# Attention of a two-layer transformer: query halves outermost, totals over three, three and two key tiles, two output buffers

## The reference

```python
scores = jnp.einsum('bhqd,bhkd->bhqk', q, k) / np.sqrt(HD)
attn = jax.nn.softmax(scores, axis=-1)
out = jnp.einsum('bhqk,bhkd->bhqd', attn, v)
x = residual + out @ wo + bo
x = x + gelu(norm(x) @ ff_w1 + ff_b1) @ ff_w2 + ff_b2
```

## Time and profile before

| | us |
|---|---|
| median of 3 runs | 4369.27 |
| lowest, highest | 4364.93, 4376.75 |
| the profiled execution, its own time | 4378.7 |
| its span, first to last instruction | 4376.9 |

### The profile page before, as it was taken

The page is one execution under the profiler, slowest core; times in us unless marked ns, Lnnn a source line. Parts: engine busy times, 40 slices in busy tenths (PEclk is TensorE's granted clock), DMA queues, the critical chain, the costliest instruction groups (busy, mean ns, idle before and its releaser), DMA issues.

```text
span 4376.9 us, 53519 instructions
## 1 busy us (share of the span) xinstructions
PE 3913.1 (89%) x20400; PEld 1527.1 (35%) x20400; DVE 2427.8 (55%) x3944; ACT 1618.2 (37%) x2807; POOL 1636.8 (37%) x907
## 2 busy tenths in 40 slices
PE   6978899898998989989899998998899898989999
PEld 4312343233432234322243223432244223432234
DVE  3756635655455644556454666366554665556652
ACT  1456313553125531255411553135521553125521
POOL 2367212573115732156410563026510563115620
PEclk9889999989999999999999999999899999999999
DMA  4232242221422123232122021311122112310112
GB/s 133 59 90 107 69 106 73 68 62 56 102 74 64 54 78 91 76 80 67 67 87 87 15 65 57 105 37 42 37 87 92 28 35 71 100 57 18 62 55 95
DMA packets 140701, 307.44 MB, mean 70 GB/s; under 512 B 20336, under 2 KB 60292, under 8 KB 139552
## 3 DMA queue, kind: packets, MB, share of 16 engines
q10 hardware_dynamic: 50944, 174.62, 12.5%
q1 hardware_dynamic: 89504, 129.40, 11.3%
HBM read 225.56 MB, written 36.72 MB: 60 GB/s over the span
## 4 chain that ended last, share of the span: by engine, by line
PE 67%; DVE 13%; DMA 8%; POOL 5%; issue 4%; ACT 2%; SPq 1%; ACTq 0%; POOLq 0%; DVEq 0%
PE ps L774 11%; PE ps L775 11%; PE ps L776 11%; PE ps L954 8%; PE ps L875 7%; PE ps L937 6%; PE ps L811 6%; DMA dcopy<-inverses 5%; DVE mcol L1434 5%; PE ps L969 3%; POOL sums L691 3%; PE ps L828 2%; DMA inverses<-inverse 2%; ACT probs L1116 1%; DVE turn L1356 1%
## 5 line engine op out<-in xcount | busy, mean ns | idle before, releaser
L691 POOL TENSOR_TENSOR sums<-probs 128x1024 f32<-128x1024 f32 x480 | 1141.9, 2392 | 1513.4 <-ACT probs L1116 998.3
L1434 DVE TENSOR_REDUCE mcol<-ps 128x1 f32<-128x512 f32 x2048 | 1284.8, 684 | 543.1 <-PE ps L875 541.3
L1116 ACT ACTIVATE probs<-ps 128x512 f32<-128x512 f32 x2048 | 1105.0, 604 | 905.2 <-PE ps L937 614.4
L937 PE MATMUL ps<-qs,ks 98*128 98x512 f16 x2048 | 800.1, 402 | 190.0 <-ACT probs L1116 188.0
L875 PE MATMUL ps<-ks,qs 97*128 97x512 f16 x2048 | 809.7, 401 | 104.3 <-DVE mcol L1434 72.2
L954 PE MATMUL ps<-probs,v_sb 128*32 128x512 f32 x4096 | 597.2, 659 | 0.0
L1262 ACT ACTIVATE sums<-ps,cols 128x512 f32<-128x512 f32 x256 | 175.8, 687 | 1127.2 <-PE ps L776 1127.2
L875 PEld LDWEIGHTS ps<-ks,qs 97*128 97x128 f16 x2048 | 205.2, 100 | 723.3 <-DVE mcol L1434 385.9
L1520 DVE CAST probs<-sums 128x512 f16<-128x512 f32 x256 | 123.7, 483 | 501.8 <-ACT sums L1262 501.3
L774 PE MATMUL ps<-aT,ring 128*128 128x512 f16 x1024 | 392.2, 383 | 0.0
L775 PE MATMUL ps<-aT,ring 128*128 128x512 f16 x1024 | 391.2, 382 | 0.0
(11 more groups left out here) (106 smaller groups left out, 3221.9 us busy)
## 6 DMA issues: line engine op xcount, KB each, us to landing
ring<-halves ACTq DMA_DIRECT2D x208, 512.0 KB, 3.4
qs<-hl SPq DMA_DIRECT2D x192, 128.0 KB, 4.0
ring<-halves SPq DMA_DIRECT2D x48, 512.0 KB, 6.1
ring<-in_weights ACTq DMA_DIRECT2D x39, 512.0 KB, 4.4
halves<-ring ACTq DMA_DIRECT2D x37, 512.0 KB, 2.9
dcopy<-inverses SPq DMA_DIRECT2D x64, 256.0 KB
ks<-hl SPq DMA_DIRECT2D x120, 128.0 KB, 4.3
probs<-in_x SPq DMA_DIRECT2D x8, 1024.0 KB, 6.7
```

Source lines behind the costliest of these rows:

```text
L691: pool.tensor_tensor(sums[:, m % SUM_SLOTS, :, :], prob(u - 2), prob(u), ALU.add).then_inc(sum_set[0].sem, 1)
L937: pe.matmul(ps[:, bank, :], ks[0:K_EXP, key_set(i, hh), key_head(i, hh, h), P * kt:P * kt + P], qs[0:K_EXP, qc, h, :], start=True, stop=Tr ...
L1116: act.activation(prob(u)[:, e, :], ps[:, w % SCORE_BANKS, :], ACT.Exp).then_inc(exp_done.sem, 1)
L1434: dve.tensor_reduce(mcol[:, blk % 2, 4 * j + qt, half:half + 1], src, AX.X, ALU.max).then_inc(n_free[0], 1)
```

## The change

- Blocks: the query half is outermost, then the head half, then the group. Output tiles 0 to 3 (queries of the first half) then need blocks 0 to 3 only, and start at step 54 instead of 55. The second head half is needed by block 2 instead of 4, the second query half by block 4: fills, rotations and stacks move accordingly. Set 0 of the keys is used until block 5, so `load_again` moves from unit 68 to 98 and the bias additions behind it.
- Sums: over key tiles 0 to 2, 3 to 5 and 6 to 7. The first addition of a slot adds two tiles, the second adds the third one in place; 10 additions a block, 80 an iteration (75 on POOL, 5 on DVE), 3 groups of totals a block, 24 an iteration.
- `ocopy` has two buffers. `normalise` comes after addition 7 of 10, ACT's `finish` after score 11 and POOL's after addition 1, both of the block after that.
- The last block's sums are inverted by DVE in `dcopy` itself, 128 x 512, with no DMA. Forward steps: output tiles 4 to 7 at 2 and 3, norm of their half at 4, finish of blocks 6 and 7 at 0 and 1.

```diff
-O_AT, D_AT, HI_AT, INVERT_AT = 7, 12, 27, 4
+PROBS, SUM_SLOTS, SUMS, GROUPS = 6, 3, 80, 24
+SUM_KT = (1, 2, 4, 5, 7)
+O_AT, D_AT, HI_AT, INVERT_AT, NORM_AT, LO_AT = 7, 12, 11, 4, 7, 1
-WO_AT = 55
-LN2_AT = 62
-BIAS_AT = (40, 41, 42, 43, 48, 49, 54, 55)
-ROTATE_AT = ((1, 2, 6), (5, 6, 16), (14, 15, 31), (26, 28, 59))
+WO_AT = 54
+LN2_AT = 61
+BIAS_AT = (62, 63, 64, 65, 66, 67, 70, 72)
+TURNS = ((("k", 1, 0), -1, 1, 5), (("k", 1, 1), 3, 4, 11), (("q", 0, 1), 13, 17, 29), (("q", 1, 1), 33, 35, 57))
 def block_of(blk):
-    hh, r = divmod(blk, 4)
-    return hh, r // 2, r % 2
+    qc, r = divmod(blk, 4)
+    return r // 2, qc, r % 2
 def sum_of(u):
-    return 8 * (u // 16) + 2 * (u % 16 // 4) + u % 2
+    return 10 * (u // 16) + 2 * (0, 0, 1, 2, 2, 3, 4, 4)[u % 16 // 2] + u % 2
 def sum_unit(m):
-    return 16 * (m // 8) + 4 * (m % 8 // 2) + 2 + m % 2
+    return 16 * (m // 10) + 2 * SUM_KT[m % 10 // 2] + m % 2
+def sum_opens(m):
+    return m % 10 // 2 != 1 and m % 10 // 2 != 3
+def sum_buffer(m):
+    return 6 * (m // 10) + 2 * (0, 0, 1, 1, 2)[m % 10 // 2] + m % 2
 def fills_of(i):
-        for step, key in ((1, ("k", i, 1, 0, 0)), (2, ("k", i, 1, 0, 1)), (3, ("v", i, 1, 0)), (4, ("v", i, 1, 1)),
-                          (5, ("k", i, 1, 1, 0)), (6, ("k", i, 1, 1, 1)), (8, ("v", i, 1, 2)), (9, ("v", i, 1, 3))):
+        for step, key in ((0, ("k", i, 1, 0, 0)), (1, ("k", i, 1, 0, 1)), (2, ("v", i, 1, 0)), (3, ("k", i, 1, 1, 0)),
+                          (4, ("k", i, 1, 1, 1)), (6, ("v", i, 1, 1)), (7, ("v", i, 1, 2)), (9, ("v", i, 1, 3))):
 def narrow_forward(i, n):
-        if n in (3, 4):
-            keys += [("wo", i, 2 * n - 2), ("wo", i, 2 * n - 1)]
+        if n in (2, 3):
+            keys += [("wo", i, 2 * n), ("wo", i, 2 * n + 1)]
...
-        ocopy = sb("ocopy", [P, D], F32)
+        ocopy = sb("ocopy", [P, 2, D], F32)
             def attention(i):
-                        if s == 9:
+                        if s == 7:
                             put_stack(("k", i, 1, 1, 0))
             def forward(i):
-                totals_out(i, 7)
-                inverse_in(i, 7)
...
             def add_probs(i, m):
-                u = sum_unit(m)
+                u, n = sum_unit(m), sum_buffer(m)
                 pool.wait_ge(exp_done.sem, exp_done.at(i, 2 * u + 2))
+                dst = sums[:, n % SUM_SLOTS, :, :]
+                if sum_opens(m):
+                    if n >= SUM_SLOTS:
+                        pool.wait_ge(d_mul.sem, d_mul.at(i, (n - SUM_SLOTS) // 2 + 1))
...
+                    pool.tensor_tensor(dst, prob(u - 2), prob(u), ALU.add).then_inc(sum_set[0].sem, 1)
+                else:
+                    pool.wait_ge(*sum_done(m - 2, i))
+                    pool.tensor_tensor(dst, dst, prob(u), ALU.add).then_inc(sum_set[0].sem, 1)
             def attention(i):
-                    if m == 56:
+                    if m == 69:
                         deviation("ln2", i, 0)
-                    if m >= 8 and m % 8 == 3:
-                        normalise(i, m // 8 - 1)
-                    if m >= 8 and m % 8 == (4 if m // 8 == 6 else 5):
-                        finish(i, m // 8 - 1)
+                    if m >= 10 and m % 10 == NORM_AT:
+                        normalise(i, m // 10 - 1)
+                    if m >= 20 and m % 10 == LO_AT:
+                        finish(i, m // 10 - 2)
             def out_tile(key):
-                pe.wait_ge(at_lo.sem, at_lo.at(i, 6 if tt < 4 else 8))
+                pe.wait_ge(at_lo.sem, at_lo.at(i, 4 if tt < 4 else 8))
             def o_copy(i, blk):
-                if 8 * i + blk >= 1:
-                    act.wait_ge(at_lo.sem, at_lo.at(i, blk))
+                if 8 * i + blk >= 2:
+                    act.wait_ge(at_lo.sem, at_lo.at(i, blk - 1))
             def attention(i):
-                    if u == 68:
+                    if u == 98:
                         load_again(i)
+            def invert_last(i):
+                dve.wait_ge(d_out.sem, d_out.at(i, 8))
+                dve.reciprocal(dcopy[:, :], dcopy[:, :]).then_inc(inv_last.sem, 1)
```

More of the change, by code:

```diff
@@ L144, in first_fills @@
         at = (10, 11, 13, 14, 16, 17, 19, 20, 12, 15, 18, 21)
-        keys = [(kind, j, 0, th, part) for kind in "kq" for th in range(2) for part in range(2)]
+        keys = [("k", j, 0, th, part) for th in range(2) for part in range(2)]
+        keys += [("q", j, hh, 0, part) for hh in range(2) for part in range(2)]
         keys += [("v", j, 0, e) for e in range(4)]
@@ L149, in first_fills @@
         keys = [("k", j, 0, 0, 0), ("k", j, 0, 1, 0)]
-        keys += [("q", j, 0, th, part) for th in range(2) for part in range(2)]
+        keys += [("q", j, hh, 0, part) for hh in range(2) for part in range(2)]
         keys += [("v", j, 0, e) for e in range(2)]
@@ L950, in values @@
                     pe.wait_ge(o_out.sem, o_out.at(i, u // 16))
-                if u == 64 and layer(i) == 0:
+                if u == 32 and layer(i) == 0:
                     pe.wait_ge(*freed(("v", i, 1, 3)))
@@ L956, in values, with totals @@
                 mm.then_inc(v_mul.sem, 1)
-            def totals(i, m):
+            def totals(i, group):
+                m, first, last = last_of(group), group % 3 == 0, group % 3 == 2
                 for k in range(2):
                     pe.wait_ge(*sum_done(m + k, i))
-                if m == 0:
+                if group == 0:
                     if i >= 1:
@@ L993, in attention @@
                         values(i, u - LAG)
-                    m = sum_of(max(u - LAG_D, 0))
-                    if u >= LAG_D and u - LAG_D == sum_unit(m):
-                        totals(i, m)
+                    for group in range(GROUPS):
+                        if u - LAG_D == sum_unit(last_of(group)):
+                            totals(i, group)
                     some(rows_at(i, s))
@@ L1101, in finish @@
                     act.wait_ge(hi_read.sem, hi_read.at(i, blk + 1))
-                    hi = act.activation(ocopy[:, :], ocopy[:, :], ACT.Identity, bias=bias_)
+                    hi = act.activation(ocopy[:, blk % 2, :], ocopy[:, blk % 2, :], ACT.Identity, bias=bias_)
                 hi.then_inc(at_hi.sem, 1)
@@ L1212, in attention @@
                             d_copy(i, blk - 1)
-                        if w % 32 == HI_AT:
-                            finish(i, blk - 1)
+                    if blk >= 2 and w % 32 == HI_AT:
+                        finish(i, blk - 2)
                     if w % 4 == 2:
@@ L1499, in attention @@
                         output_sum(i - 1, 3 + s)
[L1500 removed]
+                    for m in range(10 * blk, 10 * blk + 10):
                         if by_vector(m) and sum_unit(m) // 2 == s:
```

142 lines of the change are left out of this document (74 added, 68 removed).

## The result

The changed kernel takes 4211.31 us (median of 4 runs, 4204.08 to 4214.03) against 4368.16 us for the kernel before beside it (4364.93 to 4376.75): ratio 0.9635, 95% interval 0.9617 to 0.9654, so 157 us faster. I had forecast 4130, a range of 4015 to 4280, and 240 us of gain. The sign, the range and the main mechanism held; a third of the gain didn't come. The profiled execution took 4214.03 us (span 4212.2) against 4378.7 before, 164.7 less.

What follows compares the result with a forecast made beforehand. It took PE to bound attention steps, except once a block POOL's wait for the DMA chain. Gains of 4 x 24 + 4 x 34 + 8 = 240 us took the profiled 4378.7 to 4138.7; it said 4130, range 4015 to 4280.

Steps and rivals of the forecast that it cites:

- Normalising late: In attention blocks, multiplying four units later removes POOL's wait for the inverse; the long last step falls from 6.77 to 2.84 us.
- Nobody waits for the moved multiplication: With the second ocopy buffer finish runs one block later; the next o_copy needs only the finish of two blocks ago.
- Fewer totals: 56 us, all on PE's path if PE stays the limit: Attention steps: 64 fewer groups of totals at 0.87 us of PE each, 56 us in all.
- the slot wait: At a plain block's second addition POOL idles 2.4 us for a slot, making about 28.8 us a block.
- Layer 1's blocks 0, 6, 7: These layer 1 blocks were put at 27.5, 32.3 and 34 us; the whole layer at 24 us less an iteration.
- Layer 0: Its eight blocks were to sum to 280 us against 314.06, 34 us less an iteration.
- The turn to the forward part: After the last block, DVE inverts in place in 4.2 us; net gain 1 us an iteration.
- DVE beside POOL: In attention, longer POOL work was charged nothing for slowing DVE; the shared-port rule would cost up to 19 us.
- A (PE alone): Rival: PE alone limits and POOL's idle time vanishes in its lag; 392 us gained, 3977 us; chance 0.12.
- B: Rival: a second slot wait and late stacks, bias and inverse in layer 0; 120 us gained, 4250 us; chance 0.13.
- C: Rival: the wait for the inverse was hidden anyway, only PE's totals count; 56 us gained, 4313 us; chance 0.07.
- D: Rival: POOL's three slot openings a block each wait 3.1 us; 92 us slower, 4461 us; chance 0.06.

Runs made afterwards that it cites:

- experiment 1: The changed kernel with POOL's normalising multiplication after addition 4 of a block instead of 7: 4367.67 us, ratio 0.9999 to the kernel before.
- Experiment 2: The kernel before (one ocopy buffer, heads outermost) with only the multiplication moved later, its remainder and output tiles shifted to make room: 4460.19 us, ratio 1.0215.
- pairs: The changed kernel with totals over pairs of key tiles again (64 additions, 32 groups an iteration), everything else kept: 4164.13 us, ratio 0.9540.
- Experiment 5: The changed kernel with DVE's ln2 norm of the first half moved behind its additions, one step later: 4222.95 us, ratio 0.9650.
- experiments 4: The changed kernel with ACT rounding layer 0's last rotated query stack after unit 59 instead of 57: 4200.38 us, ratio 0.9605.
- experiment 6: The changed kernel with layer 0's maxima of block 2 starting at step 9 instead of 8 and run denser after: 4208.98 us, ratio 0.9616.
- 12: Pairs with later rotation, tiles apart and later maxima, plus layer 1's output tiles at steps 51, 52, 53, 55 and POOL's deviation one addition earlier: 4146.73 us, ratio 0.9484.
- experiment 7: The changed kernel with output tiles 0 to 3 in steps 53, 55, 56, 57 instead of 54 to 57: 4188.49 us, ratio 0.9570.
- experiment 8: The changed kernel with DVE's four output sums in layer 1's block 0 at steps 0, 3, 3, 6 instead of 1 to 4: 4212.90 us, ratio 0.9639.

## Why the forecast was right in sign and its gain half too large

**Normalising late: right.** L742 idles 2.5 us for the broadcast (I allowed 80), the 6.77 step is gone, plain blocks took 26.75, 28.18 and 27.88 against 28.8. By experiment 1 it is worth 157 us, the whole difference of the two kernels. What the order of the blocks and the second buffer bring by themselves wasn't tried.

**"Nobody waits for the moved multiplication": right, but my reason was incomplete.** I named the o_copy. Experiment 2 shows that ACT's finish, whose move in the diff I hadn't costed, is the nearer waiter: 303.5 us.

**"Fewer totals: 56 us, all on PE's path if PE stays the limit": wrong, with its sign.** The condition failed. I had computed 26.5 us of work for POOL against 26.1 for PE and added the slot wait, and so charged POOL's period in plain blocks; there it fits. But I kept the 56 us as a gain and read the extra additions only there. With pairs a plain block is 26.8, so the grouping *costs* 1.1 to 1.4 us in blocks 4 and 5, where it was modelled, and gains nothing in block 2. In blocks 0, 6 and 7, where other work stands in fixed places, it costs 2.0 to 3.8: -67 against -106 us in layer 1. The comparison I should have made is not with the kernel before, but with the late multiplication without the grouping: POOL's 21.0 us hide under PE's 26.5, its 25.5 don't. That the time still fell into the range, with a term of the wrong sign in the sum, is due to the range's width.

**Layer 1's blocks 0, 6, 7: each 3 to 4 us short.** They have work of other engines in fixed places (output sums, tiles, norm). I took 27.5, 32.3 and 34. In block 7 "34" had POOL waiting for the statistics, which it does (3.33 us for L1355 in the trace), but PE's long gap, 4.23 us, came through DVE: the norm ahead of an addition, itself drawn out beside POOL's additions (1.91 us before, 4.75 now). Experiment 5 shows that the order on DVE alone doesn't give it back.

**Layer 0: -59 us where I had -136, the largest miss.** One iteration took 302.93 us where I had 280. Block 0 is 50.98 (47), block 1 41.98 (37), block 3 38.83 (33), block 7 39.49 (35): the rotations "move but don't grow" was true of their length and false of their effect, since behind more additions they are late. Only block 6 was better than I said (32.91 against 37). The late key stack, which I gave 1 us, cost 5.04 us of PE where block 2's maxima want it, at the end of block 0 (I had looked for it, as a sign of being wrong, at block 2 itself). That the extra additions are part of the layer's loss is shown by the pairs, -81 against -59. But experiments 4, 5, 6 and 12 also show that such a gap is not worth its length: about half of it or more returned in the next steps, and only experiment 7 kept most of what it won.

**The turn to the forward part: -29 us over seven turns where I had -8 over all.** The inversion takes 3353 ns; I took 4.2 us for it between 0.53 and 4.2, and the place was right. From the last scores to the next iteration's first the time fell from 239.6 to 236.3 us in layer 1, some 3.4 us instead of 1. Which part of it brings this wasn't tried apart. The 8 us at the start I hadn't costed: the diff moves POOL's wait for the constant rows behind its first builds, and POOL's first root starts at 10.35 us instead of 27.02.

**DVE beside POOL: I charged nothing.** A row shows 2.75 us instead of 0.68 where they meet, as the earlier trace rows had hinted for another operation, and DVE's norm in block 7 4.75 instead of 1.91. The Trainium skill (SBUF — State Buffer, "SBUF: two separate sides") says that two such instructions hold the ports in turn, and the trace agrees: DVE's long additions end some 0.55 us after POOL's, all 18 of them in experiment 8. The sum that I worked out by that rule was 221 against 240 us; it was the nearer one, but it counted only the eight more additions on DVE. Experiment 8 puts the collision at under 1 us in block 0. The norm reads only one tile, so the rule as I put it leaves it out; its collision, up to 26 us by ACT's wait, is where I should have looked, and its price wasn't tried apart.

**The rivals.** A (PE alone) fell: POOL is in the chain. B's form, stacks and rotations late in layer 0, is what happened there (68 us of gain by its count, 59 measured), without the second slot wait in layer 1, so the time lies between B and the forecast. (Its 13 us an iteration for layer 1 don't follow from its own condition: 24 less the 6.6 to 8.5 that blocks 2, 4 and 5 lose is 16 to 18, and the whole some 4235.) C fell by experiment 1, which has fewer totals and no gain. The Trainium skill (Perfetto Trace Analysis, "Identifying the Most-Contended Engine") says to optimise the engine with the highest occupancy first. That is PE here, at 89%, and taking work from it, the totals, is just what brought nothing; what held 157 us was POOL, in order and at 37%, that stood once a block and so made PE stand. D fell, though the grouping did cost what it described in kind.

## What to carry to other kernels

When a change has two parts, price each against the kernel with the other part in it, not against the kernel before: here the change without the grouping gave 205 us, and the grouping took 41 of them back. A wait that is moved goes to the next engine in order that reads the result, so list the waiting instruction of each engine before you move it; a second buffer is what lets all of them move. And a stall of PE once a block costs its length and the lower clock in the same step, while of five stalls taken away one at a time four came back by about half or more in the next steps. Last, compare the durations of one instruction with the other elementwise engine idle and at work: an instruction that takes 1.9 us in one place takes 4.8 in another.

## What the runs showed of the hardware

- The clock's share of a stall: in layer 1 the same 154 matmuls took 26.6 us of PE at a granted clock of 1.00 and 28.2 at 0.92 (experiment 1), the same 122 24.62 us at 0.94 and 27.27 at 0.84 (experiment 6). The granted clock is at one of two levels, 1.2 and 2.4 GHz (shares of 0.5 and 1.0 in the traces), and these are means of the two over a block.
- A two-input DVE addition of 128x512 took 0.68 us with POOL idle, and up to 2.83 beside POOL's additions, ending some 0.55 us after the one that ran when it started in all 18 cases of experiment 8. A DVE norm of four 128x512 tiles (one input from a tile) took 1.91 us with POOL idle, 4.75 beside POOL, and 5.92 where more of POOL's additions ran beside it; a 128x4 instruction of DVE took 0.16 and 2.31.
- DVE's reciprocal took 0.53 us for 64 columns (on 32 partitions) and 3.35 for 512 (on 128): (3353 - 531) / 448 = 6.3 ns a column.
- POOL's addition of 128x1024 in place took 2413 ns in the mean, into a third buffer 2393.
